# A fused attention and low-rank-expert layer on one core: pair 3, the output copy, A's loads and row 5's sum moved in the written order

## What is computed

```python
def xattn(q, k, v, Wq, Wk, Wv, Wo, bo, g):          # q = layernorm(x), k = v = ctx
    qh = softmax(heads(Wq @ q), axis=-2) * 64**-0.5  # over a head's 64 channels
    kh = softmax(heads(Wk @ k), axis=-1)             # over the 1024 positions
    context = einsum('bhdn,bhen->bhde', kh, heads(Wv @ v))
    out = Wo @ einsum('bhde,bhdn->bhen', context, qh) + bo
    return out / norm(out, axis=1) * g * sqrt(128)

def ffn(x, A, B, Wr):                                # x = layernorm(x), rows of 1024
    scores = x @ Wr.T                                # 64 experts
    G = scatter(softmax(top_k(scores, 16)))
    h = einsum('nd,krd->nkr', x, A) * G[:, :, None]  # rank 16
    return einsum('nkr,kdr->nd', h, B) * 2.0

x = x + tanh(g_xattn) * xattn(layernorm(x), ctx, ctx, ...)
x = x + tanh(g_ffn) * ffn(layernorm(x), A, B, Wr)
```

## Time and profile before

| | us |
|---|---|
| median of 3 runs | 907.29 (906.74 to 909.43) |
| the profiled execution's own time | 906.83 |
| its span, first to last instruction | 905.1 |
| PE busy in the span | 882.1 (97%) |
| DVE busy | 742.8 (82%) |
| ACT busy | 678.4 (75%) |
| POOL busy | 543.8 (60%) |

### The profile page before, as it was taken

One profiled execution on the slowest core, in us unless ns is written; L12 is line 12 of the kernel. 1 busy time (PEld: TensorE's weight loads), 2 busy tenths in 40 slices (PEclk: granted clock), 3 DMA queues, 4 the chain that ended last, 5 costly groups with the idle time before them and its releaser, 6 DMA issues.

```text
span 905.1 us, 15780 instructions
## 1 busy us (share of the span) xinstructions
PE 882.1 (97%) x4604; PEld 742.8 (82%) x4604; DVE 742.8 (82%) x1515; ACT 678.4 (75%) x1392; POOL 543.8 (60%) x374
## 2 busy tenths in 40 slices
PE   6899999999999999999999899999999999999998
PEld 4677877888888888888877788889899989999996
DVE  5899899899889989998897878887778778877642
ACT  4877887788778777877886758588888878888731
POOL 3697797799899989988899956232222212222100
PEclk9999999999999999999999999999999999999999
DMA  4434645654674557354632894212221212211001
GB/s 162 164 102 156 211 139 162 213 177 166 185 239 153 180 164 227 122 164 162 192 103 94 293 347 147 70 70 71 71 71 71 71 59 75 76 65 52 24 24 47
DMA packets 46846, 120.88 MB, mean 134 GB/s; under 512 B 5712, under 2 KB 21072, under 8 KB 46800
## 3 DMA queue, kind: packets, MB, share of 16 engines
q1 hardware_dynamic: 41040, 99.37, 32.9%
q0 software_dynamic: 5472, 20.45, 7.1%
q10 hardware_dynamic: 288, 0.52, 0.2%
HBM read 87.82 MB, written 32.51 MB: 133 GB/s over the span
## 4 chain that ended last, share of the span: by engine, by line
PE 67%; DVE 10%; POOL 9%; issue 7%; ACT 5%; DMA 2%; DVEq 0%; POOLq 0%; ACTq 0%
PE ps L61 20%; PE ps L62 19%; PE ps L63 19%; PE ps L1579 4%; PE ps L1570 3%; ACT h_raw L835 3%; PE ps L1560 2%; POOL qe L490 1%; DMA aT_hi<-in_AT 1%; POOL xn_lo L456 1%; POOL ctxT_lo L449 1%; POOL qhalf L475 1%; POOL x L570 1%; POOL qe L485 1%; POOL qT_lo L495 1%
## 5 line engine op out<-in xcount | busy, mean ns | idle before, releaser
L567 POOL TENSOR_TENSOR rb<-u_in,rb 128x1024 f32<-128x1024 f32 x14 | 33.7, 2405 | 216.0 <-DVE rb L1060 216.0
L61 PE MATMUL ps<-aT_hi,yT_hi 128*128 128x448 f32 (+2 forms) x360 | 119.4, 332 | 2.0 <-DVE hg L1220 1.4
L62 PE MATMUL ps<-aT_hi,yT_lo 128*128 128x448 f32 (+2 forms) x360 | 118.1, 328 | 0.0
L63 PE MATMUL ps<-aT_lo,yT_hi 128*128 128x448 f32 (+2 forms) x360 | 118.0, 328 | 0.0
L835 ACT ACTIVATE h_raw<-hg 32x256 f32<-32x256 f32 x248 | 103.1, 416 | 17.3 <-DVE hg L1253 14.5
L835 ACT ACTIVATE y_raw<-u_in 32x256 f32<-32x256 f32 x216 | 89.5, 415 | 7.0 <-DVE u_in L1236 4.6
L61 PE MATMUL ps<-bT_hi,hT_hi 128*128 128x512 f32 x240 | 93.7, 390 | 0.0
L62 PE MATMUL ps<-bT_hi,hT_lo 128*128 128x512 f32 x240 | 93.5, 390 | 0.0
L63 PE MATMUL ps<-bT_lo,hT_hi 128*128 128x512 f32 x240 | 93.4, 389 | 0.0
L490 POOL TENSOR_TENSOR qe<-qe,qrec 128x1024 f32<-128x1024 f32 x48 | 91.3, 1902 | 1.4 <-DVE qrec L1082 1.4
L731 ACT ACTIVATE qe<-ps 128x1024 f32<-128x1024 f32 x48 | 49.1, 1024 | 42.1 <-PE ps L1560 42.1
(11 more groups left out here) (186 smaller groups left out, 2671.5 us busy)
## 6 DMA issues: line engine op xcount, KB each, us to landing
x_in<-in_x SPq DMA_DIRECT2D x16, 512.0 KB, 4.3
ctx_in<-in_ctx SPq DMA_DIRECT2D x16, 512.0 KB, 5.6
ctxT_in<-in_ctxT SPq DMA_DIRECT2D x16, 512.0 KB, 4.3
ctxT_hi<-in_ctxT POOLq DMA_DIRECT2D x16, 512.0 KB, 3.7
turn_q_scratch<-qe SPq DMA_DIRECT2D x16, 512.0 KB, 2.6
qe<-turn_q_scratch SPq DMA_DIRECT2D x64, 128.0 KB, 2.9
u_scratch<-osb SPq DMA_DIRECT2D x16, 512.0 KB, 2.9
x<-in_x SPq DMA_DIRECT2D x15, 512.0 KB, 4.0
```

The lines of the kernel that those rows point to most:

```text
L61: nc.tensor.matmul(psum, whi, mhi, start=start, stop=False)
L62: nc.tensor.matmul(psum, wlo, mhi, start=False, stop=False)
L63: return nc.tensor.matmul(psum, whi, mlo, start=False, stop=stop)
```

## The change

On ACT the output copy `out_o(b - 1, 0)` moves from ahead of the exponential of pair 2 to behind key block 3, in all elements. The body of element 0 is put in another order on all four engines: the fold of the weights follows the first shift, pair 3 (`mm_q(0, 3)`, `max_q(0, 3)`, `exp_q(0, 3)`) comes ahead of key block 0 of element 1, and the load and split of ctxT come earlier on POOL. In element 1 DVE takes `max_q(1, 0)`, `lo_kc(0)` and `max_k(1, 1)` ahead of the turn and the statistics. In element 14 `lo_kc` comes ahead of the first norm steps. In element 15 `scale_first(1)` moves back on ACT, DVE's sums, spread and statistics are put in another order, and on POOL `halve(15, 2)` and A's last five loads go ahead of `normalise(15, 1)` and of row 1's spread, and `add_first(1)` goes behind the normalisations of the pairs 2 and 3. In the second stage the sums of row 5 stand late, for which PE's pass i = 1 is written out, and in row 1 DVE's statistics come ahead of `lo_moved_h(1)`.

The diff, cut to its core (lines 580 to 626 of before are POOL, 868 to 950 ACT, 1319 to 1492 DVE, 1721 on PE):

```diff
@@ -580,11 +580,16 @@
...
         normalise(b - 1, 2)
+    if head and not started(b):
+        hi_c(b)
...
         halve(b, 0)
+    if head and not started(b):
+        lo_c(b)
...
     if tail and not head:
+        add_first(1)
@@ -608,22 +614,20 @@
...
         halve(b, 1)
-        lo_c(b)
-    if head and not ahead:
-        spread_first(1)
+        if started(b):
+            lo_c(b)
...
         lo_xn(b + 1, 0)
-    if head:
         normalise(b, 1)
-    if head and not ahead:
+        halve(b, 2)
+    elif head:
+        halve(b, 2)
...
             hi_a(t)
-    if head:
-        halve(b, 2)
+        normalise(b, 1)
+        spread_first(1)
...
         early_newton()
-    if head and not ahead:
-        add_first(1)
@@ -868,7 +872,7 @@
...
 def body(b, head, tail, ahead, early=False):
-    if tail:
+    if tail and not (isinstance(b, int) and b == 1):
@@ -925,25 +935,23 @@
...
         hi_q(b - 1, 3)
+    if head:
+        exp_q(b, 2)
+        hi_k(b, 2)
+    if ahead and not started(b):
+        hi_k(b, 3)
+        hi_xn(b + 1, 0)
+        exp_q(b, 3)
+        exp_k(b + 1, 0)
+    elif ahead:
+        hi_xn(b + 1, 0)
+        exp_k(b + 1, 0)
+    if head and started(b):
+        hi_k(b, 3)
+    if tail and head:
+        out_o(b - 1, 0, early)
...
         scale_first(1)
-    if tail and head:
-        out_o(b - 1, 0, early)
-    if head:
-        exp_q(b, 2)
-        if not started(b):
-            act.wait_ge(fold_done, 1)
-            for par in range(2):
-                nc.scalar.activation(wvo[0][:, :, par * P:par * P + P],
-                                     psX[:, par, :].rearrange("p (j o) -> p j o", o=P),
-                                     ACT.Copy, scale=DH ** -0.5).then_inc(fold_hi, 1)
-    if head:
-        hi_k(b, 2)
-    if ahead:
-        hi_xn(b + 1, 0)
-        exp_k(b + 1, 0)
-    if head:
-        hi_k(b, 3)
@@ -1319,23 +1327,27 @@
...
         std(b + 1, range(5))
-    if tail:
+    second = isinstance(b, int) and b == 1
+    if tail and head:
         sum_q(b - 1, 2)
+    if second:
+        max_q(b, 0)
+        lo_kc(b - 1)
+        max_k(b, 1)
...
         stats(b + 1)
-    if ahead and started(b):
...
         sum_q(b - 1, 3)
-    if head and started(b):
+    if head and started(b) and not second:
         max_q(b, 0)
+    if tail and not second:
+        lo_kc(b - 1)
...
         early_guess()
-    if tail:
-        lo_kc(b - 1)
-    if head and started(b):
+    if head and started(b) and not second:
@@ -1381,29 +1393,34 @@
...
         spread(2, rb, n_newton, 4 * NEWTON)
+    if last:
+        sum_q(b, 1)
...
         nc.vector.reciprocal(krec[:, :], ksum[:, :]).then_inc(k_rec, 1)
+    if ahead and started(b):
+        max_k(b + 1, 0)
+    if head:
+        lo_k(b, 2)
...
         spread(1, rb_first[1], n_newton, 4 * NEWTON)
-    if ahead:
-        max_k(b + 1, 0)
-    if head:
-        lo_k(b, 2)
...
         low_fold()
-    if last:
-        stats2_sums(0, 0)
-    if head:
-        sum_q(b, 1)
-    if last:
-        std2(0, range(4))
-    if head:
...
         max_q(b, 3)
-    if last:
-        std2(0, range(4, NCH + 1))
+        sum_q(b, 1)
+        max_k(b + 1, 0)
+    elif head and not last:
+        sum_q(b, 1)
+        lo_k(b, 3)
+        max_q(b, 3)
+    elif last:
+        lo_k(b, 3)
+        max_q(b, 3)
+        sum_q(b, 2)
+        stats2_sums(0, 0)
+        std2(0, range(NCH + 1))
@@ -1487,9 +1504,12 @@
...
             route_step(2, n)
+    if norms:
+        stats2_sums(b + 2, (j + 3) % SLOTS)
+    if first:
...
     if norms:
-        stats2(b + 2, (j + 3) % SLOTS)
+        std2(b + 2, range(NCH + 1))
@@ -1721,6 +1741,8 @@
...
         shift_q(b, 0)
+        if not started(b):
+            fold_weights()
@@ -1754,15 +1774,20 @@
...
         output(b - 1, 0, range(CH - 1, CH))
-    if ahead:
+    if ahead and started(b):
...
         tr_k(b, 2, next(turn))
+    if head and not started(b):
+        mm_q(b, 3)
...
         tr_k(b, 3, next(turn))
+    if head and started(b):
         mm_q(b, 3)
+    elif head:
+        mm_k(b + 1, 0)
@@ -1780,7 +1805,7 @@
...
     norms = not isinstance(i, int) or b <= NB - 3
-    late = isinstance(i, int) and b in (1, 2, 4)
+    late = isinstance(i, int) and b in (1, 2, 4, 5)
@@ -1792,7 +1817,9 @@
...
     ffn_body(0, j)
-with pe.Fori(1, NB // SLOTS - 1) as i:
+for j in range(SLOTS):
+    ffn_body(1, j)
+with pe.Fori(2, NB // SLOTS - 1) as i:
```

More of the change, by code:

```diff
@@ L598, in body @@
                     normalise(b, 0)
-                    hi_c(b)
+                    if started(b):
+                        hi_c(b)
                     if turned(b):
@@ L896, in body @@
                     exp_k(b, 1)
+                    if not started(b):
+                        act.wait_ge(fold_done, 1)
+                        for par in range(2):
+                            nc.scalar.activation(wvo[0][:, :, par * P:par * P + P],
+                                                 psX[:, par, :].rearrange("p (j o) -> p j o", o=P),
+                                                 ACT.Copy, scale=DH ** -0.5).then_inc(fold_hi, 1)
                 if tail:
@@ L1740, in body @@
                     shift_q(b, 1)
-                    if not started(b):
-                        fold_weights()
                 if tail and not (head and turned(b)):
```

1 line of the change is left out of this document (added).

## The result

The changed kernel takes 911.22 us (median of 5 runs, 910.24 to 912.17), where the kernel before took 907.29 (905.6 to 909.43). The ratio is 1.0045, with a 95% interval of 1.0027 to 1.0063: slower by 0.45%, where I had forecast 903.8. So the profiles show a loss of 5.4 us in the span, and 3.9 to 5.4 is what has to be explained.

A forecast was written before the change was run, and what follows sets the result against it. TensorE, busy 97% at full clock, was taken as the bound, so only its waits could be won. +0.3 - 1.55 - 0.5 - 1.25 = -3.0 us from the profiled 906.83 gave 903.8, range 900.7 to 906.0.

The forecast's parts named there:

- Last element (-0.5 us): Element 15: context(15) starts earlier, but output(15,0) waits for POOL's mt_lo and comes only 0.5 us earlier.
- 518.5 to 521: Element 15: window in us for x_second's landing; a landing outside it was to show the prediction wrong.
- x_second queues for long: Rival, element 15: x_second lands at 525.3, 5.5 us later, giving 909.3 us; chance 0.04.
- First element (+0.3): Element 0: context(0) starts 3.05 us earlier, but DVE's idle time brings max_q(1,1) 0.2 to 0.4 us later; +0.3 us.
- bound of +1.0: First element: upper bound in us, if TensorE had to wait for mt and again for exp_k.
- Output copy (-1.55): Elements 1 to 3: moving ACT's output copy behind key block 3 saves 0.51 us each, -1.55 us in all.
- Rows 5 and 9 (-1.25): Second stage: row 5's late sum removes TensorE's 1.51 us gap, 1.37 is left, and row 9's stall moves along; -1.25 us.
- 0.9 as the sign: Second stage, sum 11: a gap of about 0.9 us was expected there.

The follow-up runs named there:

- e1: Kernel before with only POOL's order in element 15 as in the change: 915.56 us, ratio 1.0069.
- e2: Changed kernel with element 15 put back to the order of before on POOL, DVE and ACT: 905.04 us, ratio 0.9964.
- e4: Changed kernel with x_second loaded into the buffer of the halves at 172 KB instead of under yT_lo: 904.57 us, ratio 0.9972.
- e5: Changed kernel with 32 unused matmuls filling TensorE's wait ahead of up(0,0) in element 15: 909.98 us, ratio to before 1.003.
- e8: Kernel before with only the output copy of the first half moved behind key block 3, in all elements: 909.25 us, ratio 1.0003.
- e3: Changed kernel with only row 1's add put back ahead of the normalisations of pairs 2 and 3: 912.59 us, ratio 1.0045.
- e15: Changed kernel with element 15 in the order of before and x_second issued early as in e12; elements 0 and 1 as changed: 904.17 us, ratio 0.9963.
- e12: e8 with SP issuing x_second right behind the put of the turned queries, before their loads back: 904.93 us, ratio 0.998.
- e16: As e15, but with elements 0 and 1 in the order of before: 903.03 us, ratio 0.9942.
- e9: Kernel before with only row 5's sums behind up(5,1), TensorE's pass i = 1 written out: 905.33 us against 906.83, ratio 0.9983.
- e14: As e15, but with element 2's statistics moved into DVE's idle time ahead of the sum of pair 2: 901.41 us, ratio 0.9937.
- e18: e15 with SP issuing b_raw's eight loads only after A's last load has landed: 904.99 us, ratio 0.9976.
- e17: e14 with SP issuing b_raw's eight loads only after A's last load has landed: 904.03 us, ratio 0.9956.
- e7: e4 with DVE's statistics of element 2 moved ahead of the sum of pair 2 of element 0: 904.63 us, ratio 0.9963.

## Why the prediction was wrong

**The step that failed is "Last element (-0.5 us)".** Its times on POOL were right: A's loads at 507.94 (forecast 508.0), the spread's end at 514.91 (514.95), POOL free at 518.62 (518.65). That they agree to 0.1 is in part luck: the forecast counts in the time of the kernel before, and element 15 began 0.50 earlier, so within the element they came 0.4 to 0.5 late. Two things were wrong. First, I followed the late add to mt_lo and output(15,0) alone. The add also frees 68 KB for yT_lo, and up(0,0) stands ahead of output(15,0) on TensorE. So the load had no shade at all: up(0,0) came at 525.57, and the term is +7.2 instead of -0.5 (e1, e2, e4). The path that I followed did not bind: mt_lo was there at 530.05, 3.25 us ahead of output(15,0). Of this 1.2 to 1.8 us are the fall of the clock in the wait (e5). Second, I had x_second landing at 519.8, and it landed at 521.8, outside the 518.5 to 521 that I had named as a sign of being wrong. That is 2.0 of the 7.2 (an estimate, by the landings alone); the rest is the wait that I missed, with its fall of the clock. The rival "x_second queues for long" had the right transfer, but the wrong path and price: it went through mt_lo and was to decide only from 523.3 on. I gave it a chance of 0.04.

**Why x_second was late.** In the changed kernel A's loads did hold it up, and as long as I had said. These are the queues from 516 to 518 us and from 518.4 to 521.8 (packets, MB, share); SP had issued x_second at 514.94:

```profile
q0 software_dynamic: 204, 0.80, 115.1%
q1 hardware_dynamic: 8, 0.00, 4.2%
...
q1 hardware_dynamic: 358, 1.34, 97.5%
q0 software_dynamic: 23, 0.04, 3.8%
```

All but 0.04 MB of A's bytes had moved by 518.4, as forecast. But from there to the landing SP's queue moved 1.34 MB, and x_second is 0.52 of it: u_scratch, u_in and b_raw, issued from 515.40 on, moved beside it. I had given x_second the engines to itself, and had set b_raw aside because it is issued behind it. That the other loads of its own queue made the 2 us is read from these windows; no run tested it. The earlier trace rows is no proof that one queue always waits for the other: in that trace the first bytes of q1 after 518.40 came at 521.69, but e8 shows both queues at half rate over 7 us. By the rule of the Trainium skill that I cited there (DMA: Bandwidth & Descriptors, Queues, rings and completion order), the queues of an engine take turns; the trace of e8 agrees, with 1.46 and 1.28 MB, and the one of the changed kernel, with 0.80 and 0.00, does not show it.

**First element (+0.3).** The chain was right: context(0) 34.75 - 15.62 = 19.13 us after the first shift (before 22.27), DVE's idle time 0.30 + 2.19 + 0.93 = 3.42 against 3.35, max_q(1,1) 0.32 later against the first shift, forecast 0.2 to 0.4, and the second shift 0.20 later. What I had not priced is that the idle time of TensorE was now in one place, 1.15 and 1.92 us within 4.3 us. The clock fell, and from the second to the third shift it took 9.60 us instead of 7.40. The term is +2.40 in this trace, outside my bound of +1.0, of which 0.3 is won back by the first shift of element 5 (-1.82 from there, where e8 has -1.51). Where the clock was at half speed for a shorter time it was less (e2, e3, e15: 46.3 to 46.4 us from the first to the third shift instead of 47.14).

**Output copy (-1.55).** Right: 31.38 and 31.40 us for the elements 2 and 3, where it was 31.89 and 31.92. Element 1 holds the first element's loss as well; e8 shows it alone, with 31.05 instead of 31.56, and -1.51 in all. Later elements: 0, as forecast. Element 14 gained 0.48 where I had 0: kc_lo ends at 453.94 instead of 455.23, and the norm step nr behind it took 0.50 us instead of 1.07, so the key maximum behind them and scale_m came 0.5 earlier too. I had taken DVE's list as the same work in another order. e12, which leaves kc_lo in its old place, keeps element 14 at 31.56 us; e16, which moves it, has 31.02.

**Rows 5 and 9 (-1.25).** Right: -1.35 in the trace, no gap at sum 7, 0.24 at sum 8 (forecast 0.3), and row 9 gives nothing back (0.54 of wait at sum 11 against 0.52 before, where I had named 0.9 as the sign). e9 alone: 1.5 between the medians.

**Taken together.** Without the failed step the sum would have been right within 1 us: e2, the change without its last element, took 905.04, and the forecast less its last element is 904.3. Some of that is luck: in e2's trace the first element costs 1.63 where I had 0.3, and the elements 1 to 4, 14 and 15 give back 0.33, 0.50 and 0.24 that I had not counted.

## What to carry to other kernels

When an instruction is moved later, look up every wait on the semaphore that it raises, not only the data that it makes: a buffer that it frees can hold back an engine that never reads its result. A transfer that is issued within a microsecond or so of another queue's large ones had no fixed duration here (4.4 to 10.6 us for x_second); put a short one that a chain needs well ahead, and price its landing by both cases. And gains stack only up to the next shared resource: here the loads of A, B and u keep the DMA engines at shares of 0.94 to 1.12 from 510 to 535 us in the kernel before, and 3.1 to 4.3 us won in the first element bought 2.8 between the medians of e15 and e14, 1.0 between e18 and e17, and nothing between e4 and e7.
